# First-layer expert outputs added to h1's rows in DRAM by accumulating scatters, in a two-layer MoE tower on one Trainium2 core

## The reference

```
h = tok(x)                         # 3-level Haar analysis, gates per band, synthesis
h = layernorm(h + attention(h))    # 16 heads -> this is h1
h = layernorm(h + moe0(h))         # 8 experts, top-2, hidden 512, relu
h = layernorm(h + attn1(h))        # cumprod(cos) per head, LN, FFN of 1024 on 16 features, LN
h = layernorm(h + moe1(h))         # 8 experts, top-1 with capacity 641, hidden 1024, gelu
```

```
gates, expert_idx = top_k(softmax(xf @ gate_w + gate_b), 2)
h   = relu(einsum('nc,ech->neh', xf, w1) + b1)
y   = einsum('neh,ehc->nec', h, w2) + b2
out = sum over the two chosen experts of gate * y
```

## Time and profile before

| | |
|---|---|
| median of 3 runs | 1665.89 us (1665.71 to 1666.65) |
| profiled execution | 1674.18 us, its span 1672.4 us |
| granted TensorE clock, mean of the span | 0.862 |
| PE busy (x6876) | 1318.6 us, 79% |
| PE weight loads | 917.2 us, 55% |
| VectorE (DVE) busy | 918.2 us, 55% |
| GpSimd (POOL) busy | 718.7 us, 43% |
| ScalarE (ACT) busy | 506.9 us, 30% |
| DMA | 135.22 MB, mean 81 GB/s |

### The profile page before, as it was taken

The page is one execution under the profiler, slowest core; times in us unless marked ns, Lnnn a source line. Parts: engine busy times, 40 slices in busy tenths (PEclk is TensorE's granted clock), DMA queues, the critical chain, the costliest instruction groups (busy, mean ns, idle before and its releaser), DMA issues. The chain is left out here.

```text
span 1672.4 us, 23326 instructions
## 1 busy us (share of the span) xinstructions
PE 1318.6 (79%) x6876; PEld 917.2 (55%) x6876; DVE 918.2 (55%) x2506; ACT 506.9 (30%) x971; POOL 718.7 (43%) x931
## 2 busy tenths in 40 slices
PE   1378778887888839999999167777777399999997
PEld 0245555554555526666666155555555266677665
DVE  6755776775767443222222378888886334444443
ACT  1024344444545402222222244433443121111111
POOL 4453263353221132222221577677764334544453
PEclk9678898889999659999999677777777699999999
DMA  6465347346675151211221532222100170110000
GB/s 154 82 114 78 69 111 125 68 64 132 136 140 117 64 173 59 64 61 65 66 61 36 168 96 97 99 67 67 45 26 13 57 282 29 33 34 28 27 20 10
DMA packets 98952, 135.22 MB, mean 81 GB/s; under 512 B 18692, under 2 KB 81807, under 8 KB 97808
## 3 DMA queue, kind: packets, MB, share of 16 engines
q1 hardware_dynamic: 79200, 94.57, 24.0%
q0 software_dynamic: 16256, 37.94, 7.6%
q10 hardware_dynamic: 3376, 1.22, 0.4%
HBM read 75.40 MB, written 35.73 MB: 66 GB/s over the span
## 5 line engine op out<-in xcount | busy, mean ns | idle before, releaser
L966 DVE TENSOR_REDUCE top_a_a<-s_bank 128x4 f32<-128x1024 f32 x128 | 156.5, 1223 | 120.9 <-PE s_bank L615 111.5
L1127 POOL DMA_INDIRECT ex<-rows_d,tile_row x72 | 72.1, 1001 | 213.8 <-PE ebank L1147 200.2
L791 ACT ACTIVATE prob_a<-s_bank 128x1024 f32<-128x1024 f32 x128 | 130.4, 1019 | 83.1 <-PE s_bank L636 80.7
L1497 PE MATMUL mbank<-w2T_m,fhT_m 128*128 128x256 f32 x512 | 152.2, 463 | 0.0
L1935 PE MATMUL ebank<-w,exT 128*128 x320 | 145.9, 599 | 0.7 <-ACT exT L1981 0.7
L1946 PE MATMUL ebank<-w,ehT 128*128 x640 | 144.9, 379 | 0.9 <-ACT ehT L1989 0.9
L1497 PEld LDWEIGHTS mbank<-w2T_m,fhT_m 128*128 128x128 f32 x512 | 118.4, 237 | 36.6 <-ACT fhT_m L1610 10.4
L1156 PE MATMUL ebank<-w,exT 128*128 x288 | 137.4, 600 | 0.6 <-ACT exT L1203 0.6
L1168 PE MATMUL ebank<-w,ehT 128*128 x576 | 136.3, 380 | 0.8 <-ACT ehT L1209 0.8
L1946 PEld LDWEIGHTS ebank<-w,ehT 128*128 128x128 f32 x640 | 118.6, 190 | 16.1 <-issue 1.6
L1248 DVE TENSOR_TENSOR eh<-ebank,b 128x512 f32<-128x512 f32 x72 | 49.8, 692 | 139.7 <-PE ebank L1156 138.9
(11 more groups left out here) (341 smaller groups left out, 2599.0 us busy)
## 6 DMA issues: line engine op xcount, KB each, us to landing
w<-in_L_ffn_W SPq DMA_DIRECT2D x16, 1024.0 KB, 8.4
qs_a<-parts_q_a SPq DMA_DIRECT2D x96, 128.0 KB
ks_a<-parts_k_a SPq DMA_DIRECT2D x96, 128.0 KB, 6.4
y_d<-ey SPq DMA_DIRECT2D x72, 128.0 KB, 1.7
w<-in_L_ffn_w SPq DMA_DIRECT2D x16, 512.0 KB, 4.9
image_a<-in_x SPq DMA_DIRECT2D x4, 1024.0 KB, 7.4
h_d<-rec_a SPq DMA_DIRECT2D x4, 1024.0 KB
x_a<-h_d SPq DMA_DIRECT2D x16, 256.0 KB, 3.7
```

The costliest lines, as they stand in the source:

```text
L791: nc.scalar.activation(prob[:, j % 4].rearrange("p g t s -> p (g t s)"), s2_bank[:].rearrange("p g s -> p (g s)"), ACT.Exp, scale=HD ** -0 ...
L966: nc.vector.tensor_reduce(top[:, j].rearrange("p g t -> p (g t)"), s1_bank[:].rearrange("p g (t s) -> p (g t) s", t=TPI), axis=AX, op=ALU. ...
L1127: pool.indirect_dma_start(out=x[j % XR][:].bitcast(I32), out_offset=None, in_=rows_d, bounds_check=E * SLOTS - 1, oob_is_err=False, in_off ...
L1497: last = nc.tensor.matmul(b[:, t * D:(t + 1) * D], hT[:, f, t * P:(t + 1) * P], w2T[:, f, :], start=False, stop=f == FC - 1)
```

## The change

1. **The rows carry more.** A row of `rows0_d` has 264 words instead of 256: the two expert numbers, the two gates and the two targets (both the token's own number). `route` writes them behind h1's tile; `rows` no longer makes two copies. `sends0` (token numbers) is made by two iotas at the start, and two memsets clear the tails.
2. **First experts.** 71 tiles instead of 72. VectorE has a new step `owner`: it compares the two expert numbers of each row with the tile's, and so picks the gate and target. `g2` multiplies the biased output by the gate in a second instruction. GpSimd's `send(j)` adds the 128 rows to `h1_d` by an indirect scatter with `compute_op=ALU.add`. It waits for the tile's output and for the landing of `send(j - 1)`, since two tiles may name the same token. GpSimd's order is load(5), send(0), load(6), send(1) and so on. `y0_d`, SP's stores and `slots` are gone. PE's L1168 waits for `biased`, the point that `y_ok` marked before. A gather also waits for `owner` of the tile four before.
3. **Middle.** No gathers, no copies of places, no gated additions: the statistics of the first layernorm come straight from the loaded `hin`. SP issues `w1n`, `b1n`, `w2n` first, then waits for `quiet1` and loads images 0 and 1, then six constants, then image 2.
4. **Last experts.** 39 tiles instead of 40.
5. **Attention.** The six memsets of `ks` move from behind `bo2` to behind `weigh_rest(0)`, ahead of the wait for the second part of the parameters.

The core of the diff:

```diff
-MOE0_TILES = 2 * TOKENS // P + E
+MOE0_TILES = (2 * TOKENS + E * (P - 1)) // P
+ROW0 = D + 8
-MOE1_TILES = TOKENS // P + E
+MOE1_TILES = (TOKENS + E * (P - 1)) // P
...
             weigh_rest(0, last=False)
+            for u in range(RING):
+                for half in (32, 96):
+                    nc.vector.memset(ks[u][half:half + 32].bitcast(F32), 1.0).then_inc(q["ks_ok"], 1)
             dve.wait_ge(q["params_1"], 16 * 4)
...
             nc.vector.tensor_tensor(bo2[:], bank[0][:, 0:D], bo[:], ALU.add).then_inc(q["bo_ok"], 1)
-            for u in range(RING):
-                for half in (32, 96):
-                    nc.vector.memset(ks[u][half:half + 32].bitcast(F32), 1.0).then_inc(q["ks_ok"], 1)
...
+                tail = h1[i % 2]
+                c.run(nc.vector.tensor_copy(tail[:, :, D:D + 2], idx_f[:]))
+                c.run(nc.vector.tensor_copy(tail[:, :, D + 4:D + 6], sends0[:, TPI * i:TPI * i + TPI, :]))
+                c.link(nc.vector.tensor_tensor(tail[:, :, D + 2:D + 4], ex[:, :, 0:2],
...
-            for j in range(count):
-                store(j)
...
+            def load(j):
                 if j >= XR:
                     pool.wait_ge(xT_ps, j - XR + 1)
+                    pool.wait_ge(own_ok, j - XR + 1)
...
+            def send(j):
+                pool.wait_ge(y_ok, j + 1)
+                if j >= 1:
+                    pool.wait_ge(y_out[(j - 1) % YR], 16 * ((j - 1) // YR + 1))
+                pool.indirect_dma_start(out=h_d, out_offset=bass.IndirectOffsetOnAxis(ap=sent_to[j % YR][:], axis=0),
+                                        in_=y[j % YR][:], in_offset=None, bounds_check=TOKENS - 1, oob_is_err=False, compute_op=ALU.add)\
+                    .then_inc(y_out[j % YR], 16)
+
+            for j in range(count + XR + 1):
+                if j < count:
+                    load(j)
+                if j >= XR + 1:
+                    send(j - XR - 1)
...
                 if j >= 2:
-                    pe.wait_ge(y_ok, j - 1)
+                    pe.wait_ge(biased, j - 1)
...
+            def owner(j):
+                u = j % YR
+                dve.wait_ge(x_in[j % XR], 16 * (j // XR + 1))
+                if j >= YR:
+                    dve.wait_ge(y_out[u], 16 * (j // YR))
+                tail = x[j % XR]
+                c.link(nc.vector.scalar_tensor_tensor(
+                    out=chosen[:], in0=tail[:, D:D + 2].unsqueeze(1).to_broadcast([P, 2, 2]), scalar=tile_sum[:, j:j + 1],
+                    in1=tail[:, D + 2:D + 6].rearrange("p (a k) -> p a k", k=2), op0=ALU.is_equal, op1=ALU.mult))
+                c.link(nc.vector.tensor_reduce(own[u][:], chosen[:], axis=AX, op=ALU.add))
+                nc.vector.tensor_tensor(sent_to[u][:], own[u][:, 1:2], outside[:, j:j + 1], ALU.max).then_inc(own_ok, 1)
...
+                nc.vector.tensor_tensor(y[u][:], bank[4 + j % 2][:, 0:D], b[:, bass.ds(e, 1), width:width + D].rearrange("p a f -> p (a f)"),
+                                        ALU.add).then_inc(biased, 1)
+                dve.wait_ge(biased, j + 1)
+                nc.vector.tensor_scalar(y[u][:], y[u][:], own[u][:, 0:1], None, ALU.mult).then_inc(y_ok, 1)
...
-                 ("T", "p"), ("XQ", "m"), ("x1g", "m"), ("qsin", "m"), ("gather0", "n2"), ("D", "p"), ...
+                 ("T", "p"), ("XQ", "m"), ("x1g", "m"), ("qsin", "m"), ("D", "p"), ...
...
+            constants()
+            sp.wait_ge(s["quiet1"], 4)
+            load(0)
+            load(1)
+            more_constants()
+            load(2)
...
-                for t in range(TPI):
-                    c.run(nc.vector.scalar_tensor_tensor(out=sum_[:, t, :], in0=yin[u][:, t, 0, :], scalar=gates0[:, TPI * i + t, 0:1],
-                                                         in1=hin[u][:, t, :], op0=ALU.mult, op1=ALU.add))
...
-                variances(0, sum_)
+                variances(0, hin[u])
```

More of the change, by code:

```diff
@@ L244, in attention @@
         sb = zone["high"]
-        h1 = [sb(f"h1_{u}", [P, TPI, D]) for u in range(2)]
+        h1 = [sb(f"h1_{u}", [P, TPI, ROW0]) for u in range(2)]
         row_i = [sb(f"row_i{u}", [P, TPI, 2], I32) for u in range(2)]
@@ L432, in _ @@
             c.run(nc.gpsimd.iota(tile_no[:], pattern=[[1, MOE0_TILES]], base=0, channel_multiplier=0, allow_small_or_imprecise_dtypes=True))
+            for k in range(2):
+                c.run(nc.gpsimd.iota(sends0[:, :, k], pattern=[[P, TILES]], base=0, channel_multiplier=1,
+                                     allow_small_or_imprecise_dtypes=True))
+            for u in range(2):
+                c.run(nc.gpsimd.memset(h1[u][:, :, D:ROW0], 0.0))
             c.run(nc.gpsimd.memset(ones[:], 1.0))
@@ L1099, in _ @@
                 load_bias(sp, 0, b, e, b_in)
-            def store(j):
-                sp.wait_ge(y_ok, j + 1)
-                sp.dma_start(y_v[j], y[j % YR][:]).then_inc(y_out[j % YR], 16)
-            for j in range(count):
-                store(j)
-                if j == 8:
-                    for one in used:
-                        sp.sem_clear(one)
+            sp.wait_ge(y_ok, 8)
+            for one in used:
+                sp.sem_clear(one)
             for u in range(YR):
@@ L1261, in _, with middle @@
                     g1(j)
+                    owner(j)
                 if j >= 1:
                     g2(j - 1)
-                if j == 2:
-                    slots()
+            dve.wait_ge(own_ok, count)
             c.reset()
             nc.vector.drain().then_inc(s["quiet1"], 1)
-    return y_out
-def middle(nc, block, a, s, ctx, zone, load_weights, load_bias, y_out, h1_d, y0_d, rows1_d, slot0, gates0, ident, before, ones, iota8, cnt,
+def middle(nc, block, a, s, ctx, zone, load_weights, load_bias, h1_d, rows1_d, ident, before, ones, iota8, cnt,
            away1, rank1, minus_half):
@@ L1370, in prefetch, with later @@
                     load_bias(sp, i // 2 - 5)
-            def load_or_constants(i):
-                load(i)
-                if i == 1:
-                    constants()
-            turns({"load": load_or_constants, "prep": prefetch})
+            def later(i):
+                if i >= RING:
+                    load(i)
+            constants()
[4 more added lines that the diff above has]
+            load(2)
+            turns({"load": later, "prep": prefetch})
             sp.sem_inc(s["quiet2"], 1)
@@ L1382, in _ @@
             c = Chain(pool, s["pool_c"])
[L1383 to L1394 removed]
+            pool.wait_ge(s["quiet1"], 4)
+            c.run(nc.gpsimd.memset(wstack[:].bitcast(F32), 0.0))
+            c.run(nc.gpsimd.iota(token[:, :, 0].bitcast(F32), pattern=[[P, TILES]], base=0, channel_multiplier=1,
+                                 allow_small_or_imprecise_dtypes=True))
+            c.link(nc.gpsimd.iota(token[:, :, 1:4], pattern=[[1, TILES], [0, 3]], base=0, channel_multiplier=TILES))
+            pool.sem_inc(q["const_ok"], 1)
             def root(i, k):
@@ L1452, in _ @@
             pe.wait_ge(s["quiet1"], 4)
+            pe.sem_inc(s["begun1"], 1)
             def prep(i):
```

125 lines of the change are left out of this document (34 added, 91 removed), and 4 rows, old and new, of the table STEPS.

## The result

The changed kernel took 1687.38 us (median of 4 runs, 1686.15 to 1692.27), the kernel before 1665.8 in the same set: ratio 1.0136, 95% interval [1.0115, 1.0158]. The change makes the kernel about 22 us slower; the forecast was 22 us faster. The profiled execution of the change took 1686.15 (span 1684.4). That of the kernel before (1674.18) lay 8 us above its own median, so the two spans differ by only 12. So attention is compared by runs, not by traces.

What follows compares the result with a forecast made beforehand. PE was taken to bound both experts' stages, a chain between engines the middle; +5.2 - 4.1 + 1.4 - 16.6 - 8.0 = -22.1 from the 1665.9 median gave 1643.8 us, range 1624 to 1715.

Steps and rivals of the forecast that it cites:

- The chain of sends: First experts: w (semaphore to issue) 0.77, L (issue to landing) 3.3, cycle C = 4.07, under 4.10 a tile; cost 0.
- rival (b): First experts: the chain of sends becomes the bound and PE starves, slower from L = 3.65; 1733, middle 1698; chance 0.28.
- The end of the stage: From the first experts' last `ey` to the middle's first instruction: 5.1 us instead of 3.7, +1.4.
- The tiles: One tile less in each experts' stage, PE-bound, counting in full: -4.1 in the first, -8.0 in the last.
- DVE's added work at no cost: First experts: `owner` and the gate multiplication, 1.7 us a tile, fit in DVE's idle 2.99; cost 0.
- The memsets: Attention: moving six memsets delays the three large weighings by 7.1 and PE's L544 by 5.7; +5.2 in all.
- The start of the middle: First statistics 8 us after opening instead of 14.0, and 3.8 less gated additions before PE's first `F1`; -9.8.
- Turn 2: Middle, second `F1`: PE idled only 1.98 before it, so the images behind gain at most -2.0 more.
- The steady turns: Middle: only the excess of the seven of 14 turns where DVE comes late to PE's logits is gained; -4.8.
- Rival (c): Middle: turns are bound by DVE and POOL, each shortens by 1.9, 24.7 instead of 4.8; 1624; chance 0.06.
- Rival (a): First experts: the addition costs the whole 1.3 again, L = 3.65, C = 4.42, +22; 1666; chance 0.12.

Runs made afterwards that it cites:

- the plain scatter's run: The changed kernel with the addition taken out of the scatter (plain overwriting writes to h1's rows): 1644.56 us, ratio 0.9903 to the kernel before.
- the run with two targets: The changed kernel with odd tiles' sends added to a second, unread DRAM tensor, each send waiting for the last but one: 1648.87 us, ratio 0.9923.
- the run with the loads first: The changed kernel with two accumulators added in the middle, memsets at their old place, image 0's loads ahead of the constants: 1643.14 us, ratio 0.9886.
- the run with fewer tiles: The kernel before with 71 and 39 tiles and nothing else changed: 1648.33 us, ratio 0.9924.
- that with the memsets: The kernel before with the six memsets moved ahead of the weighings and nothing else: 1667.13 us beside 1662.75, ratio 1.0035.

## Why the prediction was wrong

**The step that failed** is the length of a send in "The chain of sends": L = 3.3, w = 0.77, C = 4.07, "just hidden", cost 0. Measured were L = 3.8 and w = 0.85, so C = 4.65 for a full tile, and 4.63 in the mean over all 71 sends, of which the last three carry no rows. By the prediction's own formula 70 x (4.63 - 4.10) = 37 us. The first two rows of the table hold it together: the stage came out 24.9 + 4.1 = 29.0 longer than 71 tiles at PE's pace, and the other 8 are the growth of the lag between `ey` and send, which is paid after the last tile. So rival (b), with the mechanism, the place and the point (L = 3.65) as it was put, is what happened; its chance was 0.28, and its size lies at the low end of its range. That the result lies inside the range given is owed to this rival alone.

The landing was mis-sized in two parts, which the runs separate:

| | issue | landing without rows | landing, 64 rows | landing, 128 rows |
|---|---|---|---|---|
| plain scatter | 1.02 | 2.1 (the last three sends) | | 2.4 |
| accumulating scatter | 1.59 | 2.8 | 3.1 (issue 1.45) | 3.8 |

I wrote that POOL's issue "is paid once" and took it as 1.0 from the gather's row. An accumulating one takes 1.59, with rows or without: +0.57 that no row of the kernel before could show. The data part of 128 rows is 3.8 - 2.8 = 1.0 against 0.3 for the plain scatter, +0.7. I had added 1.0 to the gather's 2.3, where 1.5 was needed: 0.1 because a plain scatter takes 2.4, 0.57 for the issue, 0.7 for the data and 0.1 that neither holds. And w, taken from a wait on PE, was 0.08 short for a wait on a DMA, as (b) had allowed: with it even L = 3.3 would have made C = 4.15. With 0.03 us between the estimate (3.30) and the bound (3.33), and bounds of 2.3 and 4.6 around it, a cost of 0 rested on nothing that a row supported.

**The end of the stage** (+1.4 forecast, +8.9 found) failed with it. When the chain is slower than PE, PE runs ahead until buffers stop it, and the sends that lag must still be made after the last tile: three of them at 3.52 us. This is no cost beside the formula's: the formula counts sends, and these are among the 71. With the chain hidden the step is near: 5.1 us from the last `ey` to the middle were forecast, and it is 3.8 in the plain scatter's run (917.3 to 921.1) and 4.4 in that with two targets.

**The tiles**: -4.1 and -8.0, found -4.1 and -7.9 in the profile, -12.6 by runs (-17 to -8). Right.

**DVE's added work at no cost**: right. The run with two targets has all of it and 4.09 a tile.

**The memsets**: +5.2, found +5.8 (2.5 to 9.3). Right, and L544 came at 39.47 where 39.6 was forecast:

```profile
39.47 0.57 PE L544 MATMUL bank<-tok_part_a,blocks_a 128*128 128x10 f32 x2 [6.49 <-DVEq L897]
```

**The start of the middle**: the first statistics 8.1 us after the stage opens, 8 forecast. From there to `F1` 23.9 were found where 22.0 were forecast. Part of the rest is a new neighbour: with the gathers gone, POOL's L1427 (1.25, at 975.00) now runs beside DVE's L1672, which took 1.73; before, POOL issued a gather there and the same operation (L1689) took 0.69. In the other 15 turns of the change no such neighbour overlaps it, and it takes 0.69. In the run with the loads first the neighbour comes later: there this operation takes 0.69 in all 16 turns, and DVE's L1646, which now runs beside it, takes 1.29 instead of 0.21. So the 1.04 go with the overlap in every trace looked at; it was not tried by itself. The other 0.9 that were forecast and not found, the additions of image 1, stay open.

**Turn 2**: -2.0 forecast, and +0.6 found (1009.81 - 992.90 = 16.9 against 983.66 - 967.32 = 16.3). Wrong: the images behind did not come nearer to the first. The 0.6 itself means nothing: with the middle of the kernel before this distance is 17.8 in the run with fewer tiles and 17.5 in that with the memsets, and 16.8 to 17.6 in the runs with the new middle. **The steady turns**: -4.8 forecast, -5.8 found over 14 turns (`F1` from 1009.81 to 1311.14, before from 983.66 to 1290.75; -7 against the two runs just named), a little more than forecast. Rival (c) fell for the reason given: DVE waits for PE's logits in 14 of 14 turns, 25.7 us in all, where it had been 5 and 6.3. Most of DVE's freed time turned into that wait. An addition of 0.69 put back on DVE in each turn cost no turn either: it still waits 14 times, 19.6 us in all, in the run with the loads first.

**The rule on two source reads** (the Trainium skill, "Collectives: The Full Stack", section "The bandwidth ceiling: the fold count and why AG ≠ RS ≠ AR"): it is stated there for large ring collectives, and applied here it would double the part of a transfer that moves data. The runs go the same way and further: 0.3 became 1.0. What the rule does not speak of, the longer issue, weighed nearly as much.

Rival (a), at L = 3.65, and the forecast differ from what was found by 0.15 and 0.5 us of landing per send; with 70 sends in a row this is 10 and 35 us.

## What to carry to other kernels

When a change puts a chain of dependent DMAs beside an engine that is full, the time of one link is everything, and an operation that no row of the trace shows has to be measured by itself before its cost is set to 0; if its bounds straddle the pace of the full engine, that is the whole forecast. Such a chain is cheaply broken in two by giving alternate links separate targets and adding them where an engine idles: 4.52 a tile became 4.09. The price was one addition a turn in a stage whose engine had time, and a second tensor that has to be filled with zeros, whose cost stays open. A single profiled execution cannot settle a difference of a few us in a stage that moves by more than this from run to run.
